# Second attention of a two-block hybrid kernel: projections and ranks at other pairs, Newton steps of the row norms on GpSimd, gathers that read the slots directly

## The reference

```python
x = x + attn_a(layernorm(x))   # linear attention with a causal mask, 16 heads
x = x + ffn(layernorm(x))      # 16 experts, top 2, a capacity for each
x = x + attn_b(layernorm(x))   # sparse attention: 6 queries of each head
x = x + ffn(layernorm(x))      # the same expert weights again
```

```python
scores = Q @ K.T * scale                      # 512 x 512 for each head
top_u  = top_k(scores.max(axis=-1), 6)[1]     # the 6 queries with the largest score
attn   = softmax(q_sel @ K.T * scale)         # for these queries alone
ctx    = attn @ V                             # scattered back to rows top_u
out    = padded @ wo.T + bo
```

## Time and profile before

| | us |
|---|---|
| median of 3 executions | 1549.39 (1541.33 to 1552.91) |
| the profiled execution | 1551.83 |
| its span, first to last instruction | 1549.5 |

### The profile page before, as it was taken

How to read it: one execution, slowest core, us unless ns; L and a number is a source line. 1 busy time by engine, 2 the same in 40 slices (tenths; PEclk the granted TensorE clock), 3 DMA queues, 4 the chain that set the end, 5 groups by cost and what they waited for, 6 DMA issues and landing times.

```text
span 1549.5 us, 28769 instructions
## 1 busy us (share of the span) xinstructions
PE 1305.2 (84%) x8534; PEld 802.8 (52%) x8534; DVE 1137.9 (73%) x5084; ACT 768.2 (50%) x1903; POOL 732.2 (47%) x1041
## 2 busy tenths in 40 slices
PE   3988888887899999999999999999999989999300
PEld 1555554454798964444444444444444448888300
DVE  3898998898473658788888889888888784755422
ACT  2343443341564766555655656556555556646200
POOL 2135555446423213354555655545554342347775
PEclk9999999999899988888988979978888889999755
DMA  6645412001354520000000000110000003557522
GB/s 171 226 140 176 139 57 75 27 24 55 112 187 155 176 83 14 10 19 26 22 23 28 29 21 21 38 60 28 29 25 18 28 29 121 162 159 229 161 80 70
DMA packets 119770, 125.82 MB, mean 81 GB/s; under 512 B 15552, under 2 KB 109888, under 8 KB 119616
## 3 DMA queue, kind: packets, MB, share of 16 engines
q1 hardware_dynamic: 103232, 90.42, 18.2%
q0 software_dynamic: 16384, 33.59, 7.5%
HBM read 50.15 MB, written 73.79 MB: 80 GB/s over the span
## 4 chain that ended last, share of the span: by engine, by line
PE 49%; DVE 27%; issue 7%; POOL 7%; ACT 5%; DMA 3%; SPq 1%; POOLq 0%; ACTq 0%; DVEq 0%
PE pair L1814 19%; DVE pT L1321 7%; PE pair L1741 7%; POOL vmyg L522 5%; DVE pT L1047 3%; PE pair L1752 3%; DVE xs L1231 3%; PE pair L1730 2%; PE pair L1605 2%; ACT pT L816 2%; PE bank L1544 2%; PE bank L1550 2%; PE bank L1842 2%; DVE st L898 2%; PE bank L1802 1%
## 5 line engine op out<-in xcount | busy, mean ns | idle before, releaser
L1814 PE MATMUL pair<-kT,apart 32*128 32x512 f32 x2048 | 480.6, 743 | 34.7 <-DVE smax L1321 33.4
L816 ACT ACTIVATE pT<-pair 128x256 f32<-128x256 f32 x1024 | 328.9, 396 | 259.0 <-PE pair L1814 257.5
L1321 DVE CUSTOM_DVE_ANT_0 pT<-pair,pT 128x256 f32<-128x256 f32 x1024 | 381.4, 417 | 100.9 <-ACT pT L816 97.4
L1814 PEld LDWEIGHTS pair<-kT,apart 32*128 32x128 f32 x2048 | 196.0, 210 | 194.7 <-DVE smax L1321 118.9
L1741 PE MATMUL pair<-xeT,unit_w 128*128 128x256 f32 x768 | 186.9, 387 | 0.0
L1047 DVE TENSOR_TENSOR pT<-pair,causal 128x512 f32<-128x512 f32 x256 | 158.4, 680 | 23.8 <-PE pair L1605 23.8
L522 POOL DMA_INDIRECT vmyg<-ybufA,slg x128 | 122.3, 955 | 84.9 <-issue 36.6
L1206 DVE TENSOR_TENSOR hid<-sg,pair 128x512 f32<-128x512 f32 x96 | 65.9, 686 | 126.3 <-ACT sg L742 125.9
L1741 PEld LDWEIGHTS pair<-xeT,unit_w 128*128 128x128 f32 x768 | 142.0, 195 | 16.0
L482 POOL DMA_INDIRECT dispB<-xnf,sli x128 | 126.5, 988 | 43.6 <-issue 43.6
L482 POOL DMA_INDIRECT dispA<-xnf,sli x128 | 126.9, 992 | 40.6 <-issue 40.6
(11 more groups left out here) (235 smaller groups left out, 2025.8 us busy)
## 6 DMA issues: line engine op xcount, KB each, us to landing
dispB<-zeros SPq DMA_DIRECT2D x16, 1408.0 KB
apart<-dispA SPq DMA_DIRECT2D x96, 128.0 KB
ybufA<-ye SPq DMA_DIRECT2D x48, 256.0 KB
apart<-dispB SPq DMA_DIRECT2D x96, 128.0 KB
ybufB<-ye SPq DMA_DIRECT2D x48, 256.0 KB
dispA<-zeros SPq DMA_DIRECT2D x33, 128.0 KB
xs<-in_x SPq DMA_DIRECT2D x16, 256.0 KB, 3.0
out<-xs SPq DMA_DIRECT2D x16, 256.0 KB, 2.5
```

Of the source, the lines that this page charges most:

```text
L816: act.activation(rel[n % RING][:, q, :], pair[n % RING][:, q, HALF:SEQ], ACT.Relu).then_inc(s["relu_done"], 1)
L1321: dve.tensor_tensor_reduce(out=rel[n % RING][:, q, :], in0=pair[n % RING][:, q, 0:HALF], in1=rel[n % RING][:, q, :], scale=1.0, scalar=LOW ...
L1814: pe.matmul(pair[n % RING][:, q, :], apart[h][at, j, t * P:(t + 1) * P], kTs[h][at, HALF:], start=True, stop=True).then_inc(s["bsc_done"], 1)
```

## The change

Four things are moved or replaced.

1. On PE the q projection goes from pair 9 to pair 17, the k projection from 17 to 23, and the rank matmuls from 21 to 14. Since they share bank 0, the q projection waits for VectorE's use of the ranks. VectorE's `route_ranks` goes from pair 21 to 16; ScalarE's four masked copies from pairs 9 to 12 to pairs 18 to 21, its keys from 18 to 24.
2. The three Newton steps of the second attention's norms are made on GpSimd, four operations a step instead of three, behind the scatters. The shift operation goes; normalised rows are `(x - mean) * rstd`, again two operations.
3. `fetch` reads its row numbers from the slot table itself; VectorE's copies `slg` go. It waits for the sums of the batch two before it (`combined`) instead of for the copy.
4. GpSimd's key differences go from ahead of the bias addition to behind the scatters.

The diff, cut to its core:

```diff
@@ gpsimd
             def fetch(g, h):
-                pool.wait_ge(s["slg_ready"], g + 1)
+                if g % HALFB in range(2):
+                    pool.wait_ge(s["slots_in"], g // HALFB + 1)
+                if g > 1:
+                    pool.wait_ge(s["combined"], g - 1)
                 settle(pool)
+                at = (g % B) * TB * K
                 for j in range(TB * K):
                     pool.indirect_dma_start(
...
-                        in_offset=bass.IndirectOffsetOnAxis(ap=slg[h][:, j:j + 1], axis=0),
+                        in_offset=bass.IndirectOffsetOnAxis(ap=slots[:, at + j:at + j + 1], axis=0),
...
+            def newton(call, W):
+                at = 11 * (call - CALLS - 2)
+                pool.wait_ge(s["rs"], rs_before(call) + 2)
+                for r in range(3):
+                    y, z = lny[r % 2], (lny[1 - r % 2] if r < 2 else rstd)
+                    if r:
+                        pool.wait_ge(s["rs_pool"], at + 4 * r)
+                    pool.tensor_tensor(lnt[:, 0:W], y[:, 0:W], y[:, 0:W], ALU.mult).then_inc(s["rs_pool"], 1)
+                    pool.wait_ge(s["rs_pool"], at + 4 * r + 1)
+                    pool.tensor_tensor(lnu[:, 0:W], lnt[:, 0:W], lnh[:, 0:W], ALU.mult).then_inc(s["rs_pool"], 1)
+                    pool.wait_ge(s["rs_pool"], at + 4 * r + 2)
+                    pool.tensor_scalar(lnt[:, 0:W], lnu[:, 0:W], 1.5, None, ALU.add).then_inc(s["rs_pool"], 1)
+                    pool.wait_ge(s["rs_pool"], at + 4 * r + 3)
+                    last = pool.tensor_tensor(z[:, 0:W], lnt[:, 0:W], y[:, 0:W], ALU.mult)
+                    last.then_inc(s["rs_pool" if r < 2 else "rstd_ready"], 1)
...
             def body(b, u, h, x, last=True, next=True, fetch_=True, before=True):
...
-                if next:
-                    key_differences(b + 1, 1 - h)
                 add_bias(b, b + B, b_bo)
                 if before:
                     places(b - 2, b - 2 + B, h)
                     send(b - 2 + B, u - 1 + B // 2, h)
+                if next:
+                    key_differences(b + 1, 1 - h)
+                if before:
                     sent(u - 1 + B // 2, h)
+                newton(b + 2 + CALLS, TB * (last + fetch_))
@@ scalar, body
-                    if next and 9 <= n < 13:
-                        masked_q(b + 1, 1 - h, range(n - 9, n - 8))
+                    if next and 18 <= n < 22:
+                        masked_q(b + 1, 1 - h, range(n - 18, n - 17))
-                    if next and n == 18:
+                    if next and n == 24:
                         keys(b + 1, 1 - h)
@@ vector, body
-                    if last and n == 0:
-                        last_newton(b - 1)
-                    if fetch and n == 1:
-                        indices(b + 2, h)
-                    if before and n == 21:
+                    if before and n == 16:
                         route_ranks(b - 2 + B, bank[0])
-                    if n in (30, 31):
-                        newton(b + 2 + CALLS, norm_width(b), (n - 30,))
@@ tensor, body
-                    if next and n == 9:
-                        project_q(b + 1)
+                    if before and n == 14:
+                        if next:
+                            pe.wait_ge(s["att_xT_ready"], b + B + 2)
+                        else:
+                            pe.wait_ge(s["ffn_xT_ready"], b + B - 1)
+                        ranks(b - 2 + B, bank[0])
                     if next and n == 17:
-                        project_k(b + 1)
+                        if before:
+                            pe.wait_ge(s["rk_done"], b + B)
+                        project_q(b + 1)
-                    if before and n == 21:
-                        if next:
-                            pe.wait_ge(s["bkT_ready"], b + 2)
...
-                        ranks(b - 2 + B, bank[0])
+                    if next and n == 23:
+                        project_k(b + 1)
```

56 lines of the change are left out of this document (21 added, 35 removed).

## The result

| | us |
|---|---|
| kernel before, median of 4 executions | 1545.36 (1532.03 to 1552.91) |
| changed kernel, median of 4 executions | 1579.19 (1576.95 to 1588.0) |
| ratio, 95% interval | 1.0239 (1.0154 to 1.0324) |
| changed kernel, the profiled execution | 1577.81, span 1575.6 |

A forecast was written before the change was run, and what follows sets the result against it. PE, VectorE and ScalarE lead by turns, with the clock falling after PE idleness. Terms of -2.85 us (9 to 16) and 12.45 against 11.01 (16 to 25) gave -1.4 a batch, -18.3 in all: 1531 us, range 1504 to 1570.

The forecast's parts named there:

- q from pair 9: In front of pair 10, the q projection leaves PE's chain and VectorE's wait vanishes: -1.05 us a batch.
- The clock from 9 to 16: Pairs 9 to 16 would mostly run at full clock, 9.64 us without q; -2.85 us a batch against the mean 12.81.
- GpSimd's new order: On GpSimd, key differences behind eight scatters come at pair 16 + 14.4 us, still in time for PE; cost 0.
- q at 17 behind the ranks: At pair 17, q waits for VectorE's ranks on shared bank 0; reduction 18 comes 1.4 us late.
- Rival C: q's wait of 1.8 us halves the clock in pairs 18 to 24, 2.9 us a batch: 1569 us; chance 0.21.
- ScalarE's backlog from 18 to 22: ReLU, four masked copies and turned exponentials keep ScalarE leading for 5.39 us; reduction 22 starts 1.1 us later.
- k at 23: The k projection waits for the last masked copy, so pair 24 reaches VectorE +0.4 to +0.5 us later.
- Newton steps and slot copies off VectorE: Behind pairs 30 to 1, 2.1 us a batch leave VectorE; taken as 0, with 2.1 as the other bound.
- Rival B: VectorE's relief counts too if the clock holds at the batch's border, up to 2.1 us a batch: 1504 us; chance 0.10.
- Rival D: Newton steps on GpSimd block VectorE, twelve times 0.24 us, 2.9 us a batch: 1569 us; chance 0.03.
- The normalised rows come at the same time: 0: GpSimd's twelve dependent operations take 3.7 to 4.2 us, about as long as VectorE's steps did: 0.
- Cover of the key differences: GpSimd's key differences finish 1.5 us or more before PE needs them at the next batch's head.

The follow-up runs named there:

- e5: Changed kernel with GpSimd's bias addition moved behind the slot arithmetic, away from the selection rows: 1532.92 us, ratio 0.9926 to the kernel before.
- e3: Changed kernel with VectorE's rank operations behind pair 13 in place of 16: 1531.14 us in the faster group, ratio 0.9888 to the kernel before.
- e7: Changed kernel with VectorE's ranks at pair 13 and the bias addition behind the slot arithmetic: 1504.12 us, ratio 0.9736 to the kernel before.
- e6: Changed kernel with VectorE's ranks at pair 13 and Newton steps and slot copies back on VectorE: median 1561.79 us, ratio 1.0141 to the kernel before.
- e2: Changed kernel with all moves undone, leaving Newton steps on GpSimd and gathers from the slots: 1588.32 us, ratio 1.028 to the kernel before.

## Why the prediction was wrong, step by step

- **q from pair 9:** forecast -1.05 us, measured -1.10. Right.
- **The clock from 9 to 16: the step that failed.** "I expect 9 to 16 to look like the full-clock batch, less q", -2.85 us; measured 12.50 against 12.81, -0.31. Where the clock held, the stretch took 9.42 to 9.92 us, and in e5, without the clash, 10.06 on the mean: the size was right. What failed is the premise that the gap behind pair 11 keeps its length. (e3, which leaves the clash and takes away q's wait by reducing the ranks earlier, has 11.51: the two are not independent.) The paragraph on GpSimd's new order asked only what comes late (the key differences) and not what comes early: the bias addition, taken out of the expert sum's company, landed beside VectorE's routing operations, on which PE waits. It was booked as a relief and never as a load. The step was mis-sized by 2.54 us a batch, 33 us in all; e5 gets 2.44 of them back.
- **q at 17 behind the ranks:** reduction 18 was forecast 3.85 us after pair 16; in a batch with the clock at 1.00 in this stretch (from 976.64) it came 4.0 after. Right at full clock; the wait of 1.8 us was forecast too. Rival C's half clock came in eight of 13 batches (14.07 us on the mean against 13.23), 0.84 us a batch; C had asked 2.9. All eight had lost the clock behind pair 11 already; in e5 three of 13 batches lose it here, and two of these had kept it behind pair 11. e3 shows that the wait's removal gives 48 us in the changed kernel, e7 against e5 that it is 29 us without the clash. So C named a true cause, and the clash, which no rival named, was the other.
- **ScalarE's backlog from 18 to 22:** 5.43 forecast, 5.52 measured. Right.
- **k at 23:** +0.4 to +0.5 forecast, +1.03 measured. The forecast let k start at the end of the last masked copy and left out ScalarE's context copy and PE's context matmul behind it, which make 0.75 us. 16 to 25 at full clock is 13.23 and not 12.45 mostly for this.
- **Newton steps and slot copies off VectorE:** 0 forecast with 2.1 as the other bound; 0 to 3 and 29 to 32 gained 0.44 together in the changed kernel, and e6 against e3 puts the whole at 1.4 a batch. Rival B was right in part, and its gain was hidden behind larger losses. Rival D, a block by the small steps, did not occur: VectorE's reductions have 418 ns on the mean in that kernel and 417 before.
- **"The normalised rows come at the same time: 0":** true, but for a reason that the prediction left unsaid. e2 shows that it hangs on the early ranks, at 4.9 us a batch.
- **Cover of the key differences:** forecast 1.5 us or more; they were done 6.3 us ahead of PE's first pair of the next batch. Right.

The sum: forecast -1.4 us a batch; add 2.54 behind pair 11, 0.78 for the pieces from 16 to 25 at full clock and 0.84 for the clock there, and it is +2.8, against +2.56 measured; most of the difference is the 0.44 gained at 0 to 3 and 29 to 32, less 0.28 lost at 3 to 9. The range missed since its case C was priced as an addition to a held first gap, and the case with both clocks lost was left out of it.

## What to carry to other kernels

When an operation is taken out of a list, follow its former neighbours: here two GpSimd operations that had been kept apart by a third met beside a chain of tiny VectorE operations on which PE waited. A term booked as relief at one place is a load at another, and both have to be priced. When waits and order are re-cut, test the pieces in both directions: each half of this change costs 2.5% or more alone, and with one number and the order of two operations set differently the whole gains 2.6%.
